# Two weight loads of an attention block requested in the middle of the head group before, not at its end

## What is computed

```python
q = (x @ Wq + bq).reshape(B, S, N_HEAD, HEAD_DIM).transpose(0, 2, 1, 3)   # S 512, 16 heads of 32
k = (x @ Wk + bk).reshape(B, S, N_HEAD, HEAD_DIM).transpose(0, 2, 1, 3)
v = (x @ Wv + bv).reshape(B, S, N_HEAD, HEAD_DIM).transpose(0, 2, 1, 3)
scores = jnp.einsum('bhqd,bhkd->bhqk', q / math.sqrt(HEAD_DIM), k) + attention_bias
probs = jax.nn.softmax(jnp.where(src_mask, -jnp.inf, scores), axis=-1)
ctx = jnp.einsum('bhqk,bhkd->bhqd', probs, v).transpose(0, 2, 1, 3).reshape(B, S, D)
x = x + (ctx @ Wo + bo)
```

## Time and profile before

| | |
|---|---|
| median of 3 runs | 5019.55 us (5014.91 to 5022.92) |
| profiled execution | 5020.92 us, of which the span of instructions is 5018.9 us |
| PE busy / DVE / ACT / POOL | 86% / 53% / 50% / 25% of the span |
| granted TensorE clock, mean | 0.933 of full speed |
| DMA | 704.31 MB, mean 140 GB/s |

### The profile page before, as it was taken

The page is one execution under the profiler, slowest core; times in us unless marked ns, Lnnn a source line. Parts: engine busy times, 40 slices in busy tenths (PEclk is TensorE's granted clock), DMA queues, the critical chain, the costliest instruction groups (busy, mean ns, idle before and its releaser), DMA issues.

```text
span 5018.9 us, 70808 instructions
## 1 busy us (share of the span) xinstructions
PE 4328.5 (86%) x25808; PEld 3077.7 (61%) x25808; DVE 2639.2 (53%) x5783; ACT 2488.5 (50%) x4700; POOL 1272.0 (25%) x637
## 2 busy tenths in 40 slices
PE   7995798888989898888989898888989898888887
PEld 3441566666757566666757576666767575666666
DVE  8981545455453646454553645454454636454553
ACT  0102454647374555646374555646374645546462
POOL 0000132231414132231414132322314142322313
PEclk9995899999999999999999999999999999999999
DMA  3323653536354544535354544535353645535351
GB/s 117 104 96 85 190 163 109 171 108 189 114 173 132 161 153 122 178 99 178 118 165 132 166 152 123 178 110 178 106 177 120 189 128 152 158 114 174 111 168 51
DMA packets 534759, 704.31 MB, mean 140 GB/s; under 512 B 45280, under 2 KB 254992, under 8 KB 534384
## 3 DMA queue, kind: packets, MB, share of 16 engines
q1 hardware_dynamic: 517520, 666.23, 44.6%
q10 hardware_dynamic: 16896, 33.56, 1.8%
HBM read 529.30 MB, written 35.72 MB: 113 GB/s over the span
## 4 chain that ended last, share of the span: by engine, by line
PE 55%; DVE 8%; SPq 7%; ACT 6%; DMA 6%; issue 5%; POOL 3%; ACTq 0%; POOLq 0%; DVEq 0%
PE bank L845 33%; PE bank L926 6%; SPq L536 6%; PE bank L890 5%; PE bank L914 4%; PE bank L949 3%; PE bank L915 3%; ACT prob L697 2%; ACT probT L718 2%; DMA w_raw<-in_L_cond_Wk 2%; DMA w_raw<-in_L_cond_Wo 1%; DVE parts L1196 1%; DMA stack<-parts 1%; PE bank L854 1%; DMA V<-in_L_cond_W 1%
## 5 line engine op out<-in xcount | busy, mean ns | idle before, releaser
L627 POOL TENSOR_TENSOR w<-w_raw,w 128x1024 fp32r<-128x1024 f32 x240 | 587.5, 2448 | 2224.8 <-ACT w L688 2093.2
L926 PE MATMUL bank<-ident,prob 128*128 128x128 f32 x4096 | 672.3, 290 | 181.8 <-ACT probT L718 173.4
L697 ACT ACTIVATE prob<-prob,low 128x512 f32<-128x512 f32 x1024 | 736.0, 719 | 176.8 <-DVE low L1117 176.8
L1196 DVE TENSOR_TENSOR parts<-gel,parts 128x512 fp32r<-128x512 f32 x256 | 261.8, 1023 | 893.4 <-ACT parts L813 893.4
L718 ACT ACTIVATE probT<-bank 128x512 f32<-128x512 f32 x1024 | 607.8, 594 | 242.8 <-PE bank L926 227.2
L926 PEld LDWEIGHTS bank<-ident,prob 128*128 128x128 f32 x4096 | 524.7, 150 | 317.4 <-ACT prob L697 190.2
L1117 DVE CUSTOM_DVE_ANT_0 prob<-bank,prob 128x512 f32<-128x512 f32 x1024 | 696.9, 681 | 0.0
L914 PE MATMUL bank<-stack 128*128 128x512 f32 x1024 | 505.7, 496 | 98.0 <-DMA stack<-parts 52.1
L1116 DVE COPY fence<-cur 128x1 f32<-128x1 f32 x1024 | 156.0, 152 | 695.5 <-PE bank L915 669.4
L845 PE MATMUL bank<-xT,stack 128*128 128x512 f32 x1920 | 492.2, 405 | 22.1 <-DVE xT L1088 11.0
L627 POOL TENSOR_TENSOR stack<-V,stack 128x1024 fp32r<-128x1024 f32 x144 | 353.0, 2453 | 595.8 <-ACT stack L688 592.2
(11 more groups left out here) (182 smaller groups left out, 5882.4 us busy)
## 6 DMA issues: line engine op xcount, KB each, us to landing
prob<-in_fside_Bx16xSxS SPq DMA_DIRECT2D x512, 512.0 KB, 4.9
stack<-parts SPq DMA_DIRECT2D x1024, 128.0 KB, 2.5
V<-in_L_cond_W SPq DMA_DIRECT2D x256, 256.0 KB, 3.6
w_raw<-in_L_cond_W SPq DMA_DIRECT2D x256, 256.0 KB, 3.0
field<-in_x SPq DMA_DIRECT2D x16, 1024.0 KB, 5.3
x<-total ACTq DMA_DIRECT2D x16, 1024.0 KB, 5.8
xin<-x SPq DMA_DIRECT2D x16, 1024.0 KB, 5.6
w_raw<-in_L_cond_Wv SPq DMA_DIRECT2D x64, 256.0 KB, 2.8
```

The costliest lines, as they stand in the source:

```text
L627: pool.tensor_tensor(w[s][:, 1, :], w_raw[s], w[s][:, 0, :].bitcast(F32), ALU.subtract).then_inc(w_lo[s], 1)
L697: act.activation(prob[:, i, :], prob[:, i, :], ACT.Exp, bias=low[:, i:i + 1], scale=-1.0, accum_out=total[:, g % 2, i:i + 1]).then_inc(exp ...
L926: mm = t.transpose(turned[e % 2][:, k * P:(k + 1) * P], prob[:, i, k * P:(k + 1) * P], ident[:])
L1196: v.tensor_tensor(parts[:, 2 * (f % 2) + 1, :], gel[:, f % 2, :], parts[:, 2 * (f % 2), :].bitcast(F32), ALU.subtract).then_inc(g_lo, 1)
```

## The change

The load of Wq/Wk of group 3 moves from behind `group(b, 0)` into its loop over p, at p = 5, ahead of that p's wait; the load of Wo's first half moves from behind `group(b, 1)` to the same place in group 1. Nothing else is touched, and every DMA remains. The diff in full:

```diff
@@ -547,6 +547,10 @@
 
                             for j in range(HG):
                                 load_stack(b, g + 1, j)
+                        if p == 5 and g == 0:
+                            load_qk(0, ITEMS[0] * b + W0_QK + 3, 3)
+                        if p == 5 and g == 1:
+                            load_rows(0, ITEMS[0] * b + W0_O, Wo, 0)
 
                         sp.wait_ge(probT_full, ENTRIES * b + entry(g, 2 * p + 1) + 1 + START)
                         load_bias(b, g + 1, p // 2, p % 2)
@@ -589,11 +593,8 @@
                     for j in range(HG):
                         load_stack(b, 0, j)
                     load_qk(0, ITEMS[0] * b + W0_QK + 2, 2)
-                    group(b, 0)
-                    load_qk(0, ITEMS[0] * b + W0_QK + 3, 3)
-                    group(b, 1)
-                    load_rows(0, ITEMS[0] * b + W0_O, Wo, 0)
-                    group(b, 2)
+                    for g in range(G - 1):
+                        group(b, g)
 
                     sp.wait_ge(pv_done, 64 * (b + 1) + START)
                     for c in range(4):
```

## The result

The change made the kernel faster: 4863.44 us median of 4 runs (4855.72 to 4871.23) against 5019.97 us for the kernel before (4 runs), a ratio of 0.9689 with a 95% interval of 0.9672 to 0.9707. That is 156.5 us less; the two profiled executions, 5020.92 and 4863.62 us, differ by 157.3. The forecast was 4883, the range 4855 to 4930.

A forecast was written before the change was run, and what follows sets the result against it. ScalarE's waits for Wk and Wo were taken to bound the kernel. Earlier stack starts in groups 1 and 2 gave 16 x 8.53 = 136 us off 5020.9, less 1.4 to the median: 4883 us, range 4855 to 4930.

The forecast's parts named there:

- What bounds the kernel: ScalarE's waits for Wk and Wo at the starts of groups 1 and 2, 86.3 and 82.6 us, lie on the path.
- Step 1: ScalarE's split in groups 1 and 2 starts 4.3 and 4.0 us earlier in the third sequence; at most 158 us gained.
- Step 2: VectorE's score steps and low parts of q and k set the stacks' start, about 6.9 us after the old load request.
- The 1.2 us that ScalarE was said to have in hand: ScalarE would finish its share of k 1.2 us before VectorE gets to k's low part.
- Step 3: Stacks set the end of groups 1 and 2, so each gains what its stacks' start gains: 136 us in all.
- The clock: Full TensorE clock expected at group starts; differing request-to-stack distances blamed on the clock, 0.51 in the fifth sequence.
- The cover of the moved load: The load moved into group 1 lands at about 27.1 us with 0.8 us to spare, costed at nothing.
- ScalarE's whole wait turns into time: Rival: TensorE's pieces close up or stack issues run faster; gain 158 us, 4861 or a little below; chance 0.14.
- Late landing: Rival: the load lands late behind stacks and bias, costing 57 us (4940), or half of that (4912); chance 0.11.
- the other two: Rivals: another wait takes the 8.5 us back, 5020, chance 0.03; delayed bias holds up VectorE, slower, 5078, chance 0.02.
- the four signs: ScalarE's weight waits gone; stacks about 6.9 us after the last bias load; stack waits 52 to some 80 us; clock 1.00.

The follow-up runs named there:

- p = 7 kernel: Both weight loads requested at p = 7 of the loop instead of p = 5 as in the changed kernel: 4914.14 us (0.9794).

## Why the prediction was right, and where it was off

**What bounds the kernel** was read rightly. The two waits of ScalarE were on the path; each load alone removes its own wait and gives 5.2 and 4.3 us a sequence.

**Step 1** holds: the split starts 0.03 us after the last projection piece, 0.33 us of idling stays (0.35 in the text), and what ScalarE gained at most was 158 us.

**Step 2** had the right mechanism and a size a little off. VectorE's chain of score step, low part, score step, low part sets the start of the stacks, behind a score step that did not move. I had it 6.49 us after the piece's end (6.92 from the request mark, which lies 0.43 before it); it is 6.23. I had added durations, but VectorE's instructions start about 0.08 us before the one ahead ends: 1130.09, 1130.69, 1131.36, 1131.97, where the sum of durations gave 0.68 to 0.75 a step. That term is 0.26 x 32 = 8 us. The 1.2 us that ScalarE was said to have in hand were too many; the p = 7 kernel shows 0.7. I had VectorE's own chain those 0.26 us too late, and on ScalarE's side I let the low part of k follow the high part at once, where it starts 0.2 us later.

**Step 3** holds: the stacks set the end of both groups, since leaving half of them out gives 76 us. One part of its sum was taken as fixed and was not: the 16 issues of a group. They averaged 11.5 and 11.3 us in groups 1 and 2 before, 11.1 in both after, 8 us in all. A weight load just ahead of them is the likely reason. Where only one was moved, group 1 took 11.2 us without a load ahead and 11.4 with it, group 2 11.1 and 11.3, and with p = 7 they are at 11.5. It is not the only thing that slows them: with the low parts first they take 11.4 with no load ahead. 136 + 8 + 8 = 152 of the measured 157; the last 5 us I have not placed. So the forecast was 20 us too high because terms were too small, and not by another mechanism.

**The clock** came back as assumed: 1.00 at the starts of the groups in the sequence where it had been 0.51. But "the distances differ because of the clock" was wrong, and the trace of before shows it. In the fifth sequence, the one of the earlier trace rows:

```profile
1704.11 0.51 SPq L517 DMA_DIRECT2D w_raw<-in_L_cond_Wk  x1
...
1710.24 1.06 ACT L688 ACTIVATE w<-w_raw 128x1024 fp32r<-128x1024 f32 x1 [6.45 <-DMA w_raw<-in_L_cond_Wk]
...
1716.07 3.68 SPq L536 DMA_DIRECT2D stack<-parts  x5
```

From split to stacks it took 5.83 us, and in the third sequence 5.67 (1157.59 - 1151.92). Over all 32 places this part stays between 5.67 and 5.85 us. What differs is how long the load took to land, 6.05 us here and 4.27 in the third, 3.7 to 6.1 over all. The long landing made the distance long and the pause long, and the low clock came behind the pause. The same holds for the spread from split to split in group 1: less ScalarE's wait before the second split, the distance averages 26.8 us both before, where the mean granted clock of the 8 us behind the split of group 1 was 0.57 to 0.79, and after, where it was 1.00. (The stacks start 0.4 us later behind the split after, and their issues take 0.4 us less; these two cancel.) So in group 1 the gain is the removed wait, and no gain from the returned clock shows. The sum did not suffer, since it took the distances as measured.

**The cover of the moved load** was worked out as 0.8 us for the load issued in group 1, the one of Wo; those 16 had 0.4 to 2.1 us to spare, 1.1 on average, and landed 5.7 to 7.1 us after their issue where I had 7.5. The 16 of Wk, issued in group 0, had 0.2 to 2.5 us. It was thin and it held. Moving further ahead gains nothing, and at p = 7, on average 3.6 us later, it costs 51 us.

**The rivals.** "ScalarE's whole wait turns into time" has the nearest number, 4861, and by luck: the stacks do start later after the split (6.2 instead of 5.8 us, 14 us over 32 places), and its number came out because the stack issues got faster at the same time and by the 5 us that I have not placed. Its "stack issues run faster with no load ahead of them" was right. Late landing did not occur at p = 5; it is what p = 7 shows. VectorE's waits for bias stayed at 1.6 us (1.4 before), and behind the split of group 2 a sequence gave back 0.3 us and not 8.5, so the other two fell.

**What would show it**: the four signs came, but for the size of one. TensorE's waits for stacks grew to 58 us and not to 80. Step 3 had 0.8 us of new waiting in group 1 of the third sequence; over the 16 sequences it was 0.26 us (4.8 to 8.9 us in all). The shorter issues, 0.4 us a group there, explain most of that, and TensorE's wait of 0.55 us for ScalarE at the start of the group may be the rest; that is argued and not shown. Group 2 has next to no new waiting (46.3 and 45.8 us).

## What to carry to other kernels

When a request stands behind a loop on a queue written out in order, its transfer time is a wait of the engine that comes next. Put it into the loop, ahead of its use by at least its landing time under load (here up to 7.6 us); being further ahead gained nothing here. To size such a gain, follow the next engine from the first instruction that did not depend on the removed wait, by starts and not by durations. And when a chain of small transfers sets the end, look at both the issue time and the DMA share before splitting it over queues. Here both were near their limit: a second queue and half the bytes gave 0 and at most 12 us, and a quarter fewer transfers, with their bytes, gave 57.

## What the runs showed of the hardware

- An SBUF to SBUF DMA of 128 KB took SP 0.60 us to issue (median of 1024 in after), and one of 64 KB about the same (10.64 us for 16), while a bias load of 512 KB from HBM took 0.47 us (median; 0.36 at the least).
- Those SBUF to SBUF transfers kept the DMA engines 0.87 busy at 193 GB/s when SP issued them all, and 0.97 busy at 227 GB/s from two queues. With half the rows each they still kept them 0.67 busy, at 102 GB/s. The bias and weight loads that follow them reach 398 GB/s at full share (1146 to 1150 us in after).
- When SP and GpSimd both issued stacks, with the DMA engines 0.97 busy, SP's issues took 1.2 us each and GpSimd's 0.53: one queue was slowed and the other kept its pace.
- Behind TensorE's pauses at the starts of groups 1 and 2 (3.28 us in the third sequence, 5.07 in the fifth) the mean granted clock of the 8 us behind the split was 0.57 to 0.79 in all 32 places before, and 1.00 in all 32 after.
